# Joined edits at the seams of a two-layer kernel: where the first taps are loaded, who reduces the statistics, and in which order the stores go out

## The reference, cut to what matters

```python
# x: [8, 4096, 512] float32
def attn(x):                       # a long convolution along l, one filter for each of 512 channels
    p = sigmoid(delta); q = 1.0 - p * sigmoid(alpha)
    kernel = p * beta * exp(arange(l) * log(q))            # [512, 16, l]
    k = einsum('dnl,dn->dl', kernel, gamma * sqrt(1/16))
    return causal_fft_conv(x, k) + x * omega
x = x + attn(layernorm(x))

def ffn(x):                        # sees the first 1024*4 = 4096 tokens; 8 experts of rank 64, 2 for each token
    xr = x.reshape(T, hs)[tok]     # tokens sorted by expert
    for e in range(8):
        h = gelu(xr @ w1A[e].T @ w1B[e], approximate=False)
        out += mask(e) * (h @ w2A[e].T @ w2B[e])
    return zeros.at[tok].add(weight * out)
x = x + ffn(layernorm(x))          # the FFN is added to batch 0 alone
```

## Time and profile before

| | |
|---|---|
| three runs | 1124.06, 1125.89, 1131.58 us; median 1125.89 |
| the profiled execution's own time | 1135.82 us |
| its span in the trace | 1134.0 us |
| granted clock of TensorE, mean | 0.942 of full speed |
| TensorE matmul busy | 930.9 us (82%) |
| VectorE, ScalarE, GpSimd busy | 817.4, 783.8, 605.4 us |

### The profile page before, as it was taken

One profiled execution on the slowest core, in us unless ns is written; L12 is line 12 of the kernel. 1 busy time (PEld: TensorE's weight loads), 2 busy tenths in 40 slices (PEclk: granted clock), 3 DMA queues, 4 the chain that ended last, 5 costly groups with the idle time before them and its releaser, 6 DMA issues. The chain is left out here.

```text
span 1134.0 us, 32989 instructions
## 1 busy us (share of the span) xinstructions
PE 930.9 (82%) x11452; PEld 750.8 (66%) x11452; DVE 817.4 (72%) x1360; ACT 783.8 (69%) x1151; POOL 605.4 (53%) x706
## 2 busy tenths in 40 slices
PE   3760888888688689999999999999988888886882
PEld 2540776767577567777777777777767777775771
DVE  7978998979689324576766666766757989896891
ACT  3872898979689544656565656565667989897890
POOL 5625986858483225566566656665655323332330
PEclk9995999989989898999999999999998999899896
DMA  9998999999999794999998879898839999999976
GB/s 319 394 401 298 260 248 241 274 233 295 289 295 317 217 277 110 278 258 293 264 271 221 236 207 234 228 232 218 207 80 267 231 220 273 244 308 291 307 173 150
DMA packets 392137, 288.01 MB, mean 254 GB/s; under 512 B 125928, under 2 KB 339592, under 8 KB 391554
## 3 DMA queue, kind: packets, MB, share of 16 engines
q1 hardware_dynamic: 348098, 212.21, 69.8%
q0 software_dynamic: 19520, 36.26, 14.6%
q10 hardware_dynamic: 24448, 38.61, 10.1%
HBM read 197.41 MB, written 100.61 MB: 263 GB/s over the span
## 5 line engine op out<-in xcount | busy, mean ns | idle before, releaser
L1471 PE MATMUL ps<-xn,wb 128*128 128x128 f32 x2048 | 275.7, 290 | 0.0
L1071 ACT ACTIVATE cen<-ps 128x1024 f32<-128x1024 f32 x156 | 155.9, 1023 | 168.8 <-PE ps L1566 161.6
L1471 PEld LDWEIGHTS ps<-xn,wb 128*128 128x128 f32 x2048 | 250.7, 200 | 17.4 <-issue 3.1
L582 POOL TENSOR_TENSOR cen<-xb,mean 128x512 f32<-128x512 f32 x128 | 142.9, 1117 | 219.4 <-DVE state L1273 166.7
L1246 DVE TENSOR_TENSOR xn<-cen,rstd 128x1024 f32<-128x1024 f32 x128 | 174.5, 1363 | 49.1 <-POOL cen L582 37.9
L1566 PE MATMUL ps<-carry,wb 64*128 64x256 f32 x1248 | 172.6, 402 | 16.0 <-DVE carry L1319 8.5
L1458 PE MATMUL ps<-xn,near 128*32 128x128 f32 x2048 | 87.9, 292 | 117.7 <-DVE xn L1246 71.9
L1581 PE MATMUL ps<-cen,xn 128*64 128x128 f32 x2496 | 160.9, 276 | 1.9 <-ACT cen L1071 1.8
L1581 PEld LDWEIGHTS ps<-cen,xn 128*64 128x64 f32 x2496 | 136.2, 137 | 39.3 <-ACT cen L1071 28.0
L1257 DVE TENSOR_TENSOR xb<-xb,ps 128x1024 f32 (+1 forms) x128 | 152.9, 1195 | 8.3 <-PE ps L1483 8.3
L975 ACT ACTIVATE wb<-wide 32x1024 f32<-32x1024 f32 x126 | 144.4, 1146 | 15.5 <-DMA wide<-taps_d 12.9
(11 more groups left out here) (173 smaller groups left out, 1272.6 us busy)
## 6 DMA issues: line engine op xcount, KB each, us to landing
xb<-L_attn_x SPq DMA_DIRECT2D x160, 512.0 KB, 10.1
out<-xb SPq DMA_DIRECT2D x72, 512.0 KB, 6.3
xb<-L_attn_x ACTq DMA_DIRECT2D x128, 256.0 KB
out<-xb SPq DMA_DIRECT2D x88, 256.0 KB, 4.6
wb<-L_ffn_w_B SPq DMA_DIRECT2D x78, 256.0 KB
wide<-taps_d SPq DMA_DIRECT2D x63, 256.0 KB
dk<-decay_d SPq DMA_DIRECT2D x63, 128.0 KB
out<-y_d SPq DMA_DIRECT2D x4, 1536.0 KB, 12.8
```

Of the source, the lines that this page charges most:

```text
L582: pool.tensor_tensor(cen[:, k, 0:QB // 2].rearrange("p b r d -> p r b d"), unit_view(pool, g, i, k)[:, :, 0:UC // 2] .rearrange("p r (b d) ...
L1071: act.activation(act_h[:, b % 2].rearrange("p f t -> p (f t)"), ps[:, 2 * (b % 2):2 * (b % 2) + 2, :].rearrange("p a t -> p (a t)"), ACT.G ...
L1471: ins = pe.matmul(ps[:, QB * k + b, d * P:(d + 1) * P], wb[:, h, k * QB + b, d, :], xn[:, k, 2 * b + d, :], start=(b > 0 and d == 0), stop ...
```

## The change

It joins several edits, all at the seams between the stages. The numbers are those of this kernel.

- **First taps.** ScalarE no longer loads the taps and decays of block 0 on its own queue. SyncE loads blocks 0 to 3 right behind the last row load, and waits for `s_keep` only after that.
- **Statistics.** GpSimd reduces the statistics of rows 0 to 111 (`first_rows`, eight chained operations, between its `keep`s 58 and 59). VectorE reduces only the last 16 rows. VectorE's reciprocal goes behind its first `centre`.
- **Sends.** The first eight `send`s go between `keep`s 41 and 55, no longer 49 to 63.
- **LAG** is 4 and no longer 6.
- **Last stores of y.** They go ahead of `load1a`, two on SyncE and two on ScalarE's queue, the latter ahead of `weights_out`.
- **Row stores.** `store_last` waits for the third gather (`s_g[h] >= 32`) and no longer for `w2b`.
- **First FFN tile.** VectorE's `rank_in_half(1)` moves behind `token_stats(2)` and `stage_out(0)`, where the other tiles have it.

```diff
-    LAG = 3 * PIECES // 8
+    LAG = PIECES // 4
...
+        NHALF = 8
+        SPL = 7 * P // 8
+        SEND0 = 5 * NL // 8
...
+            def first_rows():
+                n = 0
+                def chain(ins):
+                    nonlocal n
+                    n += 1
+                    ins.then_inc(s_half, 1)
+                    pool.wait_ge(s_half, n)
+                st = stats1[:, 0:SPL, :].rearrange("p r f -> p f r")
+                m, v, r = (a[:, 0:SPL] for a in (mean, var, rstd))
+                pool.wait_ge(s_free, SPL // LR)
+                chain(pool.tensor_tensor(m, st[:, 1, :], st[:, 4, :], ALU.add))
+                chain(pool.tensor_scalar(m, m, 0.5, None, ALU.mult))
+                chain(pool.tensor_tensor(r, st[:, 1, :], st[:, 4, :], ALU.subtract))
+                chain(pool.tensor_tensor(r, r, r, ALU.mult))
+                chain(pool.tensor_scalar(r, r, D / 4.0, None, ALU.mult))
+                chain(pool.tensor_tensor(r, r, st[:, 2, :], ALU.add))
+                chain(pool.tensor_tensor(r, r, st[:, 5, :], ALU.add))
+                chain(pool.tensor_scalar(v, r, 1.0 / D, None, ALU.mult))
...
             for n in range(NL):
                 keep(n)
+                if n == SPL // LR + 2:
+                    first_rows()
...
-                if n >= NL - 2 * SENT and n % 2 == 1:
-                    send((n - (NL - 2 * SENT)) // 2)
+                if SEND0 <= n < SEND0 + 2 * SENT and n % 2 == 1:
+                    send((n - SEND0) // 2)
...
-            sp.wait_ge(s_keep, NL)
             for k in range(TB):
                 sp.wait_ge(s_tapd[k], 16 * (NK // TB))
...
                 if g == 0:
-                    for k in range(1, WB):
+                    for k in range(WB):
                         load_weights(k, k)
+                    sp.wait_ge(s_keep, NL)
...
             tiles(0)
-            sp.wait_ge(s_xn, 2 * NK)
-            sp.dma_start(load1a, w1a.rearrange("(m p) d -> p m d", p=P)).then_inc(s_wl1, 16)
...
-            for j in range(YP):
+            for j in range(0, YP, 2):
                 store_part(0, DG - 1, j, slice(P // 2, P), s_put[j])
+            sp.wait_ge(s_xn, 2 * NK)
+            sp.dma_start(load1a, w1a.rearrange("(m p) d -> p m d", p=P)).then_inc(s_wl1, 16)
...
             up_load(1, 1)
-            sp.wait_ge(s_w2b, 32)
+            for h in range(2):
+                sp.wait_ge(s_g[h], 32)
             for j in range(YP):
                 store_last(j)
...
-            act.wait_ge(s_tab, 16)
-            for k in range(TB):
-                act.wait_ge(s_tapd[k], 16 * (NK // TB))
-            act.wait_ge(s_dec, 16 * NK)
-            for k in range(1):
-                row = taps_d[k:k + 1].rearrange("k s i d -> k (s i d)")
-                src = bass.AP(row.tensor, row.offset, [[2, ZR], [2 * (P + ZR), SB], [1, 2 * P]])
-                act.dma_start(taps_in[k * ZR:(k + 1) * ZR], src).then_inc(s_w[k], 16)
-                act.dma_start(dk[:, k, :], decay_d[k:k + 1].rearrange("k s n d -> (k s) (n d)")).then_inc(s_dk[k], 16)
...
+                if g == 0:
+                    act.wait_ge(s_half, NHALF)
...
+            act.wait_ge(s_ev, UT * DG)
+            for j in range(1, YP, 2):
+                r0 = tile_half(0, NK - 1) * P + j * PR
+                act.dma_start(y_d[0:T].rearrange("(c s) d -> s c d", s=P)[:, j * PR:(j + 1) * PR, D - P // 2:D],
+                              xb_row[:, r0:r0 + PR, P // 2:P]).then_inc(s_put[j], 16)
             weights_out(0, FC + KC)
...
-            for _ in statistics(0, stats1):
+            for _ in statistics(0, stats1, SPL):
                 pass
-            dve.wait_ge(s_std, 1)
-            dve.reciprocal(rstd[:, 0:P], rstd[:, 0:P]).then_inc(s_dv, 1)
-            dve.wait_ge(s_dv, DV_STATS)
...
+            dve.wait_ge(s_half, NHALF)
             centre(0, 0, 0)
+            dve.wait_ge(s_std, 1)
+            dve.reciprocal(rstd[:, 0:P], rstd[:, 0:P]).then_inc(s_dv, 1)
+            dve.wait_ge(s_dv, DV_STATS)
...
-                if first:
-                    rank_in_half(1)
                 if is_in(q, NQ - 2):
                     token_stats(q + 2, k)
...
-                if is_in(q, NQ - 1) and not first:
+                if is_in(q, NQ - 1):
                     rank_in_half(q + 1)
```

More of the change, by code:

```diff
@@ L191, in build @@
         w1bs = wb_row[:, KC * ER:].rearrange("p (k f) -> p k f", k=2)
+        stats1 = wb_row[:, KC * ER:KC * ER + 6 * P].rearrange("p (r f) -> p r f", f=6)
         act_h = cen_row.rearrange("p (k f t) -> p k f t", k=2, t=QT)
@@ L265, in build @@
         s_dv = sem("s_dv")
+        s_half = sem("s_half")
         s_std = sem("s_std")
@@ L514, in routing_rest @@
                 assert n == NROUTE, n
+            def first_rows():
[16 more added lines that the diff above has]
+                chain(pool.tensor_scalar(v, r, 1.0 / D, None, ALU.mult))
+                assert n == NHALF, n
             rest = routing_rest()
@@ L1092, in _ @@
         def _(dve):
-            stats1 = wb_row[:, KC * ER:KC * ER + 6 * P].rearrange("p (r f) -> p r f", f=6)
             def row_stats(q, bufs=range(LBUF)):
@@ L1130, in keep2, with statistics @@
                                 ring2[:, i:i + 2, 0:P]).then_inc(s_free2, 1)
-            def statistics(g, st_of):
+            def statistics(g, st_of, r0=0):
                 n = g * DV_STATS
@@ L1140, in chain @@
                     dve.wait_ge(s_dv, n)
-                st = st_of.rearrange("p r f -> p f r")
-                m, v, r = (a[:, g * P:(g + 1) * P] for a in (mean, var, rstd))
+                st = st_of[:, r0:, :].rearrange("p r f -> p f r")
+                m, v, r = (a[:, g * P + r0:(g + 1) * P] for a in (mean, var, rstd))
                 yield chain(dve.tensor_tensor(m, st[:, 1, :], st[:, 4, :], ALU.add))
```

## The result

| | median of 20 runs, us | lowest to highest |
|---|---|---|
| before | 1126.95 | 1120.40 to 1131.58 |
| changed | 1130.41 | 1127.04 to 1134.89 |

The ratio is 1.0033, with a 95% interval of 1.0021 to 1.0045. The changed kernel is slower by a third of a per cent, some 3.7 us by the ratio and 3.5 by the medians, where I had forecast 0.9 us less. The profiled execution of the changed kernel took 1132.09 us (span 1130.3) and lies 1.7 us above its median; the one of before lay 8.9 us above its own. So their spans can't be set against each other, but the instants at the seams can.

The account below looks back on a forecast made before the run. No engine is full (TensorE busy 82%), so what ends last at four seams was taken to bound it: +0.2 - 1.0 - 0.6 + 0.5 = -0.9 us, from 1125.89 to 1125.0 us, range 1115 to 1131.

Parts of the forecast that it names:

- seam 1: End of the row loads up to the first `stage`: +0.2 us, bounds 2.7 of gain to 2.2 of loss.
- Rows land at 107.1 - 1.6 = 105.5: Last row load: lands 1.6 us earlier because 384 KB of taps and decays leave the row phase.
- the taps follow at the 240 GB/s or so: Behind the last row load: 256 KB of taps take 1.1 us more at that rate.
- W: Instant when ScalarE starts on the taps (first `reverse`): forecast 106.6 us, with `stage` at W + 7.8 = 114.4.
- bound 108.6: Latest ScalarE start allowed, with rows no earlier and taps taking 1.5 us: 2.2 us of loss.
- Rows no earlier: Worst case for the row landing, behind the latest ScalarE start of 108.6 us and 2.2 us of loss.
- The sign on record for being wrong: Profile signs against the forecast; the one meant here is row loads that land as late as before.
- Rival (c): Taps become the end of stage 1: slower than before from W = 107.5 on, 1128 to 1129 us; chance 0.15.
- Seam 2: Tile boundaries, loads for each half's fourth tile: LAG saves 0.5 us at each of two, -1.0; bounds -4 to +3.
- rival (b): Fourth tiles' loads come in time, removing 12.3 us of stall: 1113 us or a little under; chance 0.06.
- Seam 3: Last stores of y up to `pick_g`: -0.6 us, chain moving from stores to ScalarE; bounds -2.3 to +0.5.
- Seam 4: First FFN tiles: stores and gather 3 leave earlier, `w1b` slice lands no earlier; +0.5 us, bounds -2 to +2.

Follow-up runs that it names:

- The first experiment: Changed kernel with ScalarE's queue loading block 0's taps and decays again, SyncE waiting for s_keep before blocks 1 to 3; 1124.30 us, ratio 0.9982.

## Why the prediction was wrong

**What failed: seam 1, "Rows land at 107.1 - 1.6 = 105.5", "the taps follow at the 240 GB/s or so", W = 106.6, bound 108.6.** Rows landed at 110.3 and W was 110.97, 4.4 us behind my value and 2.4 past the bound. I had priced the taps' bytes, as a queue of work that comes after the rows and leaves them alone. They don't wait for the rows: a landing is recorded in 16 steps, and those of the last row load run from 100.85 to 110.26 (before from 103.19 to 107.06), while the first packets of the taps start at 100.27, ahead of all of them. So the gain that I forecast is there in the first step (2.3 us earlier) and is more than lost in the last one, since the row packets still under way take 166 ns and not 85. That packets into one half of the partitions crowd the ways into SBUF that the late rows need too is the explanation that fits all of this; which DMA engine did what isn't recorded here. "Rows no earlier" was my worst case; later than before was not in it, because I took the stretch at a share of 0.32 as free room. That the rows pay for it is shown by plain data into 32 partitions (rows at 113.0) against the same into 128 (108.25), and into 0 to 63 (112.2) against 32 to 95 (108.2).

**The rest of seam 1 was right.** From W the chain took 7.6 us, forecast 7.8: the dummy root starts at 117.03, right behind the table load. The further drain of 1.38 us that the Trainium skill (ScalarE: Activation LUTs, "What ACT_TABLE_LOAD costs") gives doesn't show now either, where the load is on the path. VectorE's eight operations took 1.7 us as forecast; GpSimd's took 4.5 (from 99.41) under the landing rows, forecast 4. VectorE waits for the root, as forecast for a late W. The sign on record for being wrong, row loads that land as late as before, was exceeded. Rival (c), given 0.15, is what happened, with its point of W = 107.5 passed by 3.5 us. Its price of 1128 to 1129 was too low: its own sum at 110.97 gives 3.5 above before's 1125.9, and 3.5 to 3.7 were measured. That the two agree so closely is partly luck, as the other seams and the experiment with one block behind the rows show.

**Seam 2, forecast -1.0 (two boundaries).** The waits fell by 1.2 us in the change's profile and by 1.3 in the mean of profiles. With the loads still late by 11 us, rival (b) was rightly turned down. In the time, LAG 4 against LAG 6 is 1146.35 against 1146.92, which can't be told from nothing.

**Seam 3, forecast -0.6.** From the end of half 0 to `pick_g` 9.0 became 8.75 us, -0.3. The chain went where I said, from the stores to ScalarE's copies and the slot table: ScalarE's copies start 1.2 us behind the last `add`, transposes 7.8 us behind it. The two queues issued in 1.2 us what had taken SyncE 6.18. The Trainium skill (DMA: Bandwidth & Descriptors, "Issuing engines are not separate DMA queues") says that a split saves just the time to issue. The trace agrees on that saving; the pure loss of 0.8 us that I drew from the page alone doesn't show, at -0.3 us.

**Seam 4, forecast +0.5, with a wrong premise.** I let the stores leave 4 us earlier and gather 3 (counted from 0, so the fourth gather) leave 6 us earlier. The stores leave later also when the 4.6 us of half 0 are taken off (413.98, before 407.69); gather 3 leaves at 417.27, before 413.53, so 0.9 us earlier by that count and not 6. The third gather shares the DMA engines with the 2 MB of `w2b` and is no earlier than these: it has landed at 413.92, `w2b` at 413.41 (before 409.41 and 407.68). From the first to the third tile's start it is 30.1 us, before 28.6. The first experiment's kernel with the FFN edits undone has 30.2, and the kernel before with only the taps moved 28.1, so those 1.5 us don't come from the edits of seam 4. The fourteen kernels that have the moved y stores spread from 28.9 to 31.7 in single profiles, mean 30.3; whether that order is the cause wasn't tried alone, and it stays open.

**The sum.** With 4.9 - 1.3 - 0.3 + 1.5 these instants give +4.8, measured +3.5 to +3.7. The single terms of a microsecond are as large as the scatter between profiles. What is settled is that the taps' new place costs some 4 to 6 us and that all other edits together lie between -4.6 and +3 us by the intervals (0.9982 and 0.9999 in the two comparisons). With the taps back on ScalarE's queue the kernel is no faster than before by any margin that the runs tell.

## What to carry to other kernels

A share of 0.32 in the last microseconds of a load phase is not free room but the tail of transfers that every consumer waits for: don't queue anything behind it that goes to partitions of one half only (0 to 63 was tried; 64 to 127 alone wasn't). When a step moves from an engine's early, slack queue to the end of another's, count its whole chain (here 7.6 us on ScalarE) from the worst landing, and put into the worst case that what stood ahead of it lands later too. Of the places tried here for the narrow load, early on a queue of its own was the best. Partitions 32 to 95 cost the rows nothing in the one run with plain data; the taps themselves weren't tried there.

## What was unexpected of the hardware

- Transfers into 32 partitions at a time, or into 0 to 63, slow those around them: 2 KB row packets take 145 to 172 ns and not 85. The DMA share reads 1.08 to 1.13 at 139 to 201 GB/s, where 128 partitions move 386 to 400 at 1.04 to 1.06. High share is no sign of high rate.
- 512 KB of it, queued after all row loads, made the last rows land 4 us later (112.24 against 108.22).
- A gather of 0.5 MB issued beside 2 MB of weights landed only some 10 us after it was issued (402.25 and 403.67, statistics at 411.73 and 413.94).
